# Group weights by one matmul per batch, reloaded from DRAM per tile, and side work in three portions

## The reference

```
logits = einsum('th,eh->te', x, gate_weight);  probs = softmax(logits)          # 32 experts
top_val, top_idx = top_k(probs, 8);            top_val /= sum(top_val)
w_tg = einsum('tk,tkg->tg', top_val, one_hot(merge_groups[top_idx], 8))         # 8 groups
h = einsum('th,goh->tgo', x, gate_up_proj[dominant_experts])                    # 8 x 384
gate, up = split(h, 2);   act = silu(gate) * up                                 # 8 x 192
out = einsum('tg,tgh->th', w_tg, einsum('tgi,ghi->tgh', act, down_proj[dominant_experts]))
```

## Time and profile before

| what | value |
|---|---|
| median of 3 runs | 1887.24 us (1886.98 to 1889.6) |
| the profiled execution | 1887.19 us, its span 1885.4 us |
| TensorE busy | 1846.4 us (98%), 9552 matmuls |
| VectorE busy | 995.9 us (53%) |
| ScalarE busy | 538.6 us (29%) |
| GpSimd busy | 323.5 us (17%) |
| DMA | 112.10 MB, 59 GB/s over the span, one hardware queue, 19.7% of 16 engines |

### The profile page before, as it was taken

The page is one execution under the profiler, slowest core; times in us unless marked ns, Lnnn a source line. Parts: engine busy times, 40 slices in busy tenths (PEclk is TensorE's granted clock), DMA queues, the critical chain, the costliest instruction groups (busy, mean ns, idle before and its releaser), DMA issues.

```text
span 1885.4 us, 24612 instructions
## 1 busy us (share of the span) xinstructions
PE 1846.4 (98%) x9552; PEld 905.6 (48%) x9552; DVE 995.9 (53%) x2036; ACT 538.6 (29%) x801; POOL 323.5 (17%) x299
## 2 busy tenths in 40 slices
PE   8799999999999999999999999999999999999999
PEld 3445554644444444444444444444444444444444
DVE  5676776754554455454436554545445455554422
ACT  3224433312221122122112233233333223333321
POOL 1123322222021120202010011111111111111111
PEclk9899999999999999999999999999999999999999
DMA  5124433333414223340310200101010101000000
GB/s 159 55 62 129 140 118 95 96 129 65 104 42 127 90 68 104 70 125 27 90 54 9 76 1 23 32 1 54 1 54 1 54 1 54 1 23 1 1 23 23
DMA packets 135830, 112.10 MB, mean 59 GB/s; under 512 B 75554, under 2 KB 92066, under 8 KB 135714
## 3 DMA queue, kind: packets, MB, share of 16 engines
q1 hardware_dynamic: 135714, 110.53, 19.7%
HBM read 78.00 MB, written 32.51 MB: 59 GB/s over the span
## 4 chain that ended last, share of the span: by engine, by line
PE 83%; issue 9%; DVE 3%; POOL 2%; DMA 2%; ACT 1%; POOLq 0%; SPq 0%; DVEq 0%; ACTq 0%
PE bank L923 44%; PE bank L1012 17%; PE bank L1092 10%; PE bank L992 4%; PE bank L932 3%; PE bank L977 1%; POOL arena L897 1%; PE bank L958 1%; PE bank L1079 1%; PE bank L1027 1%; POOL arena L871 0%; PE bank L1054 0%; DVE arena L1278 0%; DMA arena<-in_L_xattn_Wkv 0%; DMA arena<-x_after_ffn 0%
## 5 line engine op out<-in xcount | busy, mean ns | idle before, releaser
L923 PE MATMUL bank<-arena 128*128 128x512 f16 x4608 | 1042.2, 380 | 8.4 <-DVE arena L1299 7.3
L923 PEld LDWEIGHTS bank<-arena 128*128 128x128 f16 x4608 | 451.1, 98 | 538.9 <-DVE arena L1299 7.8
L1012 PE MATMUL bank<-arena 128*128 128x512 f16 x1536 | 352.1, 379 | 1.2 <-DVE arena L1506 1.2
L1092 PE MATMUL bank<-arena 128*128 128x512 f16 x1152 | 264.3, 379 | 0.9 <-POOL arena L897 0.9
L1648 DVE SCALAR_TENSOR_TENSOR arena<-bank,arena 128x512 f32<-128x512 f32 x96 | 72.0, 750 | 329.0 <-PE bank L923 329.0
L1191 ACT ACTIVATE arena<-bank,arena 128x512 f32<-128x512 f32 x128 | 99.5, 778 | 493.5 <-PE bank L923 490.5
L1012 PEld LDWEIGHTS bank<-arena 128*128 128x128 f16 x1536 | 150.1, 98 | 181.1 <-DVE arena L1506 1.7
L897 POOL TENSOR_TENSOR arena<-arena 128x512 f16<-128x512 f32 x96 | 111.0, 1157 | 626.0 <-ACT arena L1228 626.0
L1504 DVE TENSOR_SCALAR arena<-arena 128x512 f16<-128x512 f32 x128 | 65.8, 514 | 281.6 <-ACT arena L1191 281.3
L1092 PEld LDWEIGHTS bank<-arena 128*128 128x128 f16 x1152 | 112.0, 98 | 128.4 <-POOL arena L897 1.4
L1506 DVE SCALAR_TENSOR_TENSOR arena<-arena 128x512 f16<-128x512 f32 x128 | 118.0, 922 | 4.6
(11 more groups left out here) (159 smaller groups left out, 1215.8 us busy)
## 6 DMA issues: line engine op xcount, KB each, us to landing
arena<-in_L_ffn_proj SPq DMA_DIRECT2D x64, 256.0 KB, 2.9
arena<-in_L_ffn_gate_up_proj SPq DMA_DIRECT2D x96, 96.0 KB, 2.0
x_after_attention<-arena SPq DMA_DIRECT2D x8, 1024.0 KB, 5.2
arena<-x_after_attention SPq DMA_DIRECT2D x8, 1024.0 KB, 5.6
x_after_ffn<-arena SPq DMA_DIRECT2D x8, 1024.0 KB, 4.3
arena<-x_after_ffn SPq DMA_DIRECT2D x8, 1024.0 KB, 6.2
arena<-in_x SPq DMA_DIRECT2D x7, 1024.0 KB, 5.5
normalised_blocks<-arena SPq DMA_DIRECT2D x28, 256.0 KB, 2.0
```

The lines of the kernel that those rows point to most:

```text
L923: m = e.matmul(bank[b][:, :], wT[l][:, c, tile * P:(tile + 1) * P], y[h][:, c, :], start=n == 0, stop=n == NPASS - 1)
L1012: m = e.matmul(bank[t][:, :], hv[h][:, 0, t * P:(t + 1) * P], w2T[l][:, j, :], start=j == 0 and i == 0, stop=j == NH - 1 and i == 2)
L1092: m = e.matmul(bank[t][:, :], hv[h][:, 0, t * P:(t + 1) * P], dnT[l][:, j, :], start=j == 0 and i == 0, stop=j == NR - 1 and i == 2)
```

## The change

- The table `onehot` (8 x 128 columns) becomes `of_group`, of which 8 columns are written. One matmul per batch, the new step `gsum`, gives the 8 groups' weights in 8 partitions. ScalarE scales them into `gsum_s`, and SP stores these 16 KB to a DRAM scratch `gscr`.
- The step `gload` (per tile, between `ue` and `mix`) loads `gw_s` from there, a group's row of 2 KB repeated over the tile's 128 partitions (or two rows over 64 each). It waits for the store, and for the product three tiles back, whose buffer it takes; the first three wait for the last `down` instead.
- `mix` on VectorE is one operation per tile and waits for its load.
- In the expert stage a side portion is taken after `ge`, after `ue` and after `dn`. Pauses are added between `scores` and `pturn` and around `rturn`; for batch 0, whose tasks run in the feed-forward stage, they stay short.
- `block_tasks` takes the statistics in two portions, norm, block and store of a tile in one, the load with the last tile, three pauses, the copies in pairs, and one pause.

```
 def block_tasks(i):
+        def stats(ts):
+            for t in ts:
+                add("stat", i, t)
+            if NT - 1 in ts:
+                add("rs", i)
+        def tile(t):
+            add("norm", i, t)
+            add("block", i, t)
+            add("bstore", i, t)
+            if t == NT - 1:
+                add("bload", i)
+        def whole(cs):
+            for c in cs:
+                add("whole", i, c)
+        return ([lambda: stats((0, 1)), lambda: stats((2, 3))] + [lambda t=t: tile(t) for t in range(NT)]
+                + [None] * 3 + [lambda: whole((0, 1)), lambda: whole((2, 3)), None])
-        return ([stats] + [lambda t=t: step(t) for t in range(NT + 1)] + [lambda: add("bload", i)]
-                + [None] * 6 + [lambda c=c: whole(c) for c in range(NC)])
...
-        return [L[0], both(split, L[1]), L[2], L[3], L[4], L[5], L[6],
-                lambda: add("scores", b, banks=1), lambda: None, lambda: add("pturn", b, banks=1),
-                lambda: add("read", b, banks=NT), *M, lambda: add("router", b, banks=1), lambda: None, lambda: None,
-                lambda: add("rturn", b, banks=1)]
+        pause = [None] * (1 if b == 0 else 2)
+        return [L[0], both(split, L[1]), *L[2:], lambda: add("scores", b, banks=1), *pause,
+                lambda: add("pturn", b, banks=1), lambda: add("read", b, banks=NT), *M,
+                lambda: add("router", b, banks=1), *pause, *pause, lambda: add("rturn", b, banks=1), *pause, lambda: add("gsum", b, banks=1)]
...
             add("ge", b, j, banks=1)
+            apart()
             add("ue", b, j, banks=1)
-            if side:
-                side.pop(0)()
-            for gg in range(j * P // INTER, ((j + 1) * P - 1) // INTER + 1):
-                if gg * INTER >= j * P:
-                    add("bw", b, gg, banks=1)
+            apart()
+            add("gload", b, j)
             add("mix", b, j)
...
-        if side:
-            side.pop(0)()
+        apart()
...
+            elif kind == "gsum":
+                b = step[1]
+                w.wait_ge(gs_ok, nth[step])
+                e.dma_start(gscr[b], gsum_s[0:NG, :]).then_inc(gs_out, 16)
+            elif kind == "gload":
+                _, b, j = step
+                m = nth[step]
+                w.wait_ge(gs_out, 16 * (b + 1))
+                if m <= 3:
+                    w.wait_ge(down_mm, DN2 * NB)
+                else:
+                    w.wait_ge(mixed, m - 3)
+                for gg in groups_of(j):
+                    rows = slice(max(gg * INTER - j * P, 0), min((gg + 1) * INTER - j * P, P))
+                    e.dma_start(gw_s[(m - 1) % 3][rows, :], gscr[b, gg].partition_broadcast(rows.stop - rows.start)
+                                ).then_inc(gw_in[(m - 1) % 3], 16)
...
-                e.matmul(bank[k][:, :], onehot[:, gg * P:(gg + 1) * P], wTs[b % 2], start=True, stop=True).then_inc(bw_mm)
+                e.matmul(bank[k][:, :], of_group, wTs[b % 2], start=True, stop=True).then_inc(gs_mm)
...
-                for gg in groups_of(j):
-                    rows = slice(max(gg * INTER - j * P, 0), min((gg + 1) * INTER - j * P, P))
-                    w.wait_ge(bw_ok, NG * b + gg + 1)
-                    of = gw_s[(NG * b + gg) % 3]
-                    e.tensor_tensor(r[rows, :], of[rows, :], m[rows, :], ALU.mult).then_inc(mixed)
+                w.wait_ge(gw_in[(n - 1) % 3], gw_landed[n - 1])
+                e.tensor_tensor(r, gw_s[(n - 1) % 3], m, ALU.mult).then_inc(mixed)
```

More of the change, by code:

```diff
@@ L408, in make_plan, with apart @@
     while side:
-        side.pop(0)()
+        f = side.pop(0)
+        if f:
+            f()
     add("xload", "E", 1)
     add("xload", "E", 2)
+    def apart():
+        f = side.pop(0) if side else None
+        if f:
+            f()
     total = NB * NR
@@ L512, in build @@
     wcat = small(NT * P // 2, F16).rearrange("p (t s) -> p t s", t=NT)
-    onehot = small(NG * P // 2, F16)
+    of_group = small(P // 2, F16)
+    gsum_s = small(TOK)
     ctr = small(NC * CTX).rearrange("p (c s) -> p c s", c=NC)
@@ L594, in build @@
     r_mm, rout, r_exp, r_turned, r_copied = (sem(n) for n in ("r_mm", "rout", "r_exp", "r_turned", "r_copied"))
-    ge_mm, silu, ue_mm, prod, bw_mm, bw_ok, mixed, m_hi, m_lo, dn_mm = (
-        sem(n) for n in ("ge_mm", "silu", "ue_mm", "prod", "bw_mm", "bw_ok", "mixed", "m_hi", "m_lo", "dn_mm"))
+    ge_mm, silu, ue_mm, prod, gs_mm, gs_ok, mixed, m_hi, m_lo, dn_mm = (
+        sem(n) for n in ("ge_mm", "silu", "ue_mm", "prod", "gs_mm", "gs_ok", "mixed", "m_hi", "m_lo", "dn_mm"))
+    gs_out, gw_in = sem("gs_out"), [sem(f"gw_in{i}") for i in range(3)]
     SOFT, ROUT = 13, 21
@@ L646, in freed @@
             return prod, n
-        assert kind == "bw"
-        return bw_ok, n
+        assert kind == "gsum"
+        return gs_ok, n
     x_slot = {("A", b): b % 3 for b in range(NB)}
@@ L696, in pieces, with groups_of @@
         return found
+    def groups_of(j):
+        return list(range(j * P // INTER, ((j + 1) * P - 1) // INTER + 1))
+    gw_landed, landed = {}, [0] * 3
+    for b in range(NB):
+        for j in range(NR):
+            m = NR * b + j
+            landed[m % 3] += 16 * len(groups_of(j))
+            gw_landed[m] = landed[m % 3]
     w_landed, landed = {}, [0] * 8
@@ L1073, in tensor_program @@
                 project(step, upT, j, yT[b % 2], ue_mm)
-            elif kind == "bw":
-                _, b, gg = step
+            elif kind == "gsum":
+                b = step[1]
                 k = bank_free(step)
-                w.wait_ge(r_copied, b + 1)
+                w.wait_ge(r_copied, n)
                 w.wait_ge(dconst, 13)
-                e.matmul(bank[k][:, :], onehot[:, gg * P:(gg + 1) * P], wTs[b % 2], start=True, stop=True).then_inc(bw_mm)
+                e.matmul(bank[k][:, :], of_group, wTs[b % 2], start=True, stop=True).then_inc(gs_mm)
             elif kind == "dn":
@@ L1216, in scalar_program @@
                              scale=inv["gate"]).then_inc(silu)
-            elif kind == "bw":
-                _, b, gg = step
-                w.wait_ge(bw_mm, n)
+            elif kind == "gsum":
+                w.wait_ge(gs_mm, n)
                 w.wait_ge(cd_ok, 1)
-                if n > 3:
-                    w.wait_ge(mixed, mix_last(n - 3))
-                e.activation(gw_s[(n - 1) % 3], bank[bank_of[step, 0]][:, :], ACT.Copy, scale=sc["kd"]).then_inc(bw_ok)
+                if n > 1:
+                    w.wait_ge(gs_out, 16 * (n - 1))
+                e.activation(gsum_s[0:NG, :], bank[bank_of[step, 0]][0:NG, :], ACT.Copy,
+                             scale=sc["kd"][0:NG, :]).then_inc(gs_ok)
             elif kind == "mix":
-                w.wait_ge(mixed, mix_value(n))
+                w.wait_ge(mixed, n)
                 if n > 3:
@@ L1228, in scalar_program @@
                 e.activation(macth_s[(n - 1) % 3][0][:, 0, :], mact_s[(n - 1) % 3], ACT.Copy).then_inc(m_hi)
[L1231 to L1244, removed]
     def vector_program(e):
@@ L1704 @@
     yscr = nc.dram_tensor("normalised_blocks", (2, TOK, D), F32, kind="Internal").ap()
+    gscr = nc.dram_tensor("group_weights", (NB, NG, TOK), F32, kind="Internal").ap()
     out = nc.dram_tensor("out", (NB, TOK, D), F32, kind="ExternalOutput").ap()
     with ExitStack() as stack:
-        build(nc, *args, xa, xb, yscr, out, stack)
+        build(nc, *args, xa, xb, yscr, gscr, out, stack)
     r = run_bass_kernel_spmd(nc, [arrays], core_ids=[0])
```

14 lines of the change are left out of this document (7 added, 7 removed).

## The result

The changed kernel takes **1921.82 us** (median of 4 runs, 1917.02 to 1924.77) against 1887.25 beside it on the same chip: 1.0177 times as long [1.0164, 1.019]. The forecast was 1908.6, in a range from 1894 to 1915: the direction held, but the time lies 13 us above the forecast and 7 us above the range.

A forecast was written before the change was run, and what follows sets the result against it. TensorE was taken to bound the kernel, with no idle time from 397 us. 1887.2 - 12.1 (matmuls) + 19.5 (boundaries) + 6.2 (change of stage) + 7.8 (clock) = 1908.6 us, range 1894 to about 1915.

The forecast's parts named there:

- Removed matmuls: Expert stage: 56 weight-spreading matmuls of 0.216 us each leave TensorE's path, -12.1 us.
- Boundaries: Five expert-stage batch boundaries: tile 1's weights land late behind SP's other traffic; TensorE stalls 5.5 + 4 x 3.5 = 19.5 us.
- Change of stage: Feed-forward to expert: tile 0's weights queue behind store and loads, 5.5 us; first turn waits for statistics, 0.7; together 6.2.
- Block tasks of the feed-forward stage: Feed-forward stage: regrouped statistics, norms, stores and copies cost TensorE 0 us, bounds 0 to +3.
- signs of being wrong: Load of tile 1 landing before T+13, waits without a clock fall (1901), or TensorE waiting in the feed-forward stage.
- The clock: Expert stage: array runs slow after each of six pauses, 6 x 1.3 = 7.8 us, bounds 0 and 12.
- Three portions: Expert stage: taking side work in three portions per tile costs 0 us, bounds -0.5 to +2.
- the rivals, the first: Boundaries: weights overtake queued loads, landing before about T+13 (T: first projection after a batch's last `dn`); 1881.4 us; 12%.
- The second: Rival, expert stage: the stalls come but the clock does not fall; 1900.8 us; 20%.
- The third: Rival, weights' loads: the broadcast is slow, 3 us per load instead of 1, 12 more; 1920 us; 7%.
- The fourth: Rival: the trade cancels, each stall about 2 us and no clock fall; within 0.2%; 3%.
- fifth: Rival: the change doesn't do what it says, a TensorE wait remains where the spreads were; no separate chance given.

The follow-up runs named there:

- loads ahead: Changed kernel with each tile's group-weight load issued two tiles earlier in SP's list: 1887.1 us, ratio 0.9998.
- the last two: Changed kernel with weight loads two tiles ahead and loads before the store at the stage change; old block tasks 1875.4 us, new ones with rate 9 1874.5 us.
- the filled kernel: Changed kernel with 16 zero-weight matmuls before the turn of token tile 2 at the five batch boundaries: 1914.9 us, ratio 1.0149.
- old block tasks: Changed kernel with only `block_tasks` put back as it was before: 1916.7 us, ratio 1.0163.
- slower weights: Changed kernel with the weight work's rate counted for 9 instead of 12 side portions per batch: 1914.4 us, ratio 1.0137.
- start only: Changed kernel with x of batch 1 and tile 0's group weights loaded ahead of the store at the change of stage: 1915.6 us, ratio 1.0150.

## Why the prediction was wrong

By its own steps, measured in the profiled execution (1917.0) unless another is named:

- **Removed matmuls, -12.1**: right. The two kernels without new pauses show 12.3.
- **Boundaries, 5.5 + 4 x 3.5 = 19.5**: 19.7 measured, 4.07 at the first and 3.78 to 4.02 at the others. The mechanism is the one given: SP's order, receipt and context before the weights; loads ahead take all five pauses away. The profile's groups gave it: the receipt waits told where SP stands, the queued landings what a small load costs behind a large one. The first boundary was overrated by 1.4 us and the others underrated by 1.7 in all, so that the sums meet so closely is luck; in other kernels with the same order they run from 3.6 to 5.7.
- **Change of stage, 5.5 + 0.7 = 6.2**: 4.84 + 1.23 = 6.07. The first term is right in kind. The second has another cause than the one told (statistics that start behind the product), so that the sum fits is luck there. SP's timeline of the kernel after:

```profile
1070.49 1.22 SPq L836 DMA_DIRECT2D arena<-group_weights  x1
1085.27 0.47 SPq L845 DMA_DIRECT2D arena<-in_ctx  x1
...
1087.05 2.27 SPq L836 DMA_DIRECT2D arena<-group_weights  x4
```

  The weights of tile 1 are issued only at 1087.05, behind context loads that wait for VectorE to have split the context before, which stood behind the late product of tile 0; then VectorE waits for them (timeline, same kernel):

```profile
1091.17 0.69 DVE L1677 TENSOR_TENSOR arena<-arena 128x512 f32<-128x512 f32 x1 [3.81 <-DMA arena<-group_weights]
```

- **Block tasks of the feed-forward stage, 0, bounds 0 to +3**: wrong, and the first step that failed. It is 5.2 us, above the bound; a wait of TensorE in this stage was one of the signs of being wrong. I asked only what the moved portions cost where they now stand. They are also the measure by which another planner moves, and that moved a once-only chain with two waits of 5 and 6 us beside GpSimd's bias adds. A mean over 100 us of the stage can't show a thing that happens once, nor the 2.5 us that TensorE waits in this stage already before.
- **The clock, 6 x 1.3 = 7.8, bounds 0 to 12**: mis-sized, the second step that failed. The rest in E is 11.8, and about 1.7 more lie behind the pause at 789. The size was taken from the two pauses of the trace, with over 3 us of slow array behind each; here, in E, three of the five slow stretches are about 7 us long. Per pause the rest is 11.8 / 6 = 2.0, in the two other kernels with all six pauses 15.4 / 6 = 2.6 and 13.7 / 6 = 2.3. With no long pause it is -0.2 to 1.4, with one 1.1 and 2.9.
- **Three portions, 0**: right for this kernel (E of 810.3 in the last two), though not for the reason that the pace is free; beside the spreads it costs 6 us.

Forecast 1908.6, + 5.2 for the block tasks, + 4.0 for the clock in E, + 0.1 for idle time, - 0.9 in A: 1917.0, the profiled execution. The median lies 4.8 us above that, and the profiled execution is the fastest of the four; the others show a mean granted clock of 0.982 to 0.985 against its 0.986. In the profiled one the clock never fell behind the fourth pause, and kernels with the same order at the boundaries have up to 3.9 us more rest and up to 3.3 us more pause. That fits, but the other executions have no trace, so where these 4.8 us lie isn't shown.

Of the rivals, the first (the loads overtake: 1881) is refuted by landings: the product that waits for the weights starts at T+15.0, after the T+13 that the rival allows. Weights' loads of both sizes with nothing ahead, four behind 1 MB traffic, and one behind 3 MB, in three windows of the kernel after (count, KB, median us from issue to landing):

```profile
arena<-group_weights SPq DMA_DIRECT2D x2, 256.0 KB, 3.2
arena<-group_weights SPq DMA_DIRECT2D x2, 128.0 KB, 2.8
...
arena<-group_weights SPq DMA_DIRECT2D x4, 128.0 KB, 4.3
...
arena<-group_weights SPq DMA_DIRECT2D x1, 256.0 KB, 9.5
```

The second (no fall of the clock: 1900.8) is refuted by the clock of 0.5 in the windows and by the filled kernel. The third (a slow broadcast) finds no support: the product started 1.1 us earlier than forecast at the first boundary, and a load with nothing ahead lands in 3.2 us. The fourth and fifth didn't occur. The bounds of the range were those of the forecast's two failing steps: with +3 for the blocks and 12 for the clock it would have reached 1916, still under the median.

## What to carry to other kernels

Put a small load that an operation needs soon ahead of every store receipt and large load in the same ordered list; a tile or two of lead cost nothing here and, with the weights' rate adapted, turned +1.8% into -0.7%. A new pause of TensorE cost more than its length: here 2.0 to 2.6 us more for each of six pauses of 3.6 to 5.6 us. Look for the slow clock in windows of a few microseconds. When side work is packed more densely, ask which other planner counts its empty slots, and what it has that happens only once.

## What the runs showed of the hardware

- Two pauses of the same length can differ wholly in what follows: 3.85 us with no fall of the clock, 3.78 us with about 7 us at 1.2 GHz. Slow stretches came in two lengths, about 3 and about 7 us.
- Matmuls with zero weights in place of a pause kept the clock up: with 16 of them (3.5 us) before the wait the granted clock stayed at 1.00 at all five boundaries, once with 3.48 us of pause left behind them. With 8 it fell three times of five, behind pauses of 3.67, 2.61 and 2.89 us, and not behind 2.88 and 3.46.
- VectorE operations took 1.39 instead of 0.74 us and 1.48 instead of 0.49 beside four GpSimd adds of 128x512 in f32; a 128x1 operation took 1.22 instead of 0.16.
- The maximum over partitions on GpSimd is 0.38 us in its row, with 5.83 us of idle before it, and VectorE waited 4.9 us for it, so the row does not show all the time until VectorE can go on.
- Profiled executions of four kernels with the same order at the boundaries (after, old block tasks, slower weights, start only) differ by up to 3.3 us in the five pauses, 19.7 to 23.1, and by up to 3.9 us in what lies behind them, 11.8 to 15.7.
